# Edge counts per node: one-hot columns of width 128 replaced by products of two digits of eight pairs each

## The reference, cut to what matters

```python
def _gcn_norm(edge_index):
    loop = jnp.arange(N)
    src = jnp.concatenate([edge_index[0], loop])
    dst = jnp.concatenate([edge_index[1], loop])
    deg = jax.ops.segment_sum(jnp.ones_like(dst, jnp.float32), dst, num_segments=N)
    dinv = deg ** (-0.5)
    norm = dinv[src] * dinv[dst]
    return src, dst, norm
...
h = h @ W
msg = h[src] * norm[:, None]
out = jax.ops.segment_sum(msg, dst, num_segments=N) + b
```

## Time and profile before

| | us |
|---|---|
| median of three runs | 5987.89 (5987.56 to 5988.58) |
| time of the profiled execution | 5985.42 |
| its span, first to last instruction | 5983.6 |
| mean granted PE clock | 0.758 of full |
| stage `edge_tables` | 0 to 54.4 |
| stage `degrees` | 54.4 to 155.4 |
| stage `first_table` | 155.4 to 204 |
| stage `gcn` | 204 to about 3340 |

### The profile page before, as it was taken

How to read it: one execution, slowest core, us unless ns; L and a number is a source line. 1 busy time by engine, 2 the same in 40 slices (tenths; PEclk the granted TensorE clock), 3 DMA queues, 4 the chain that set the end, 5 groups by cost and what they waited for, 6 DMA issues and landing times. The chain is left out here.

```text
span 5983.6 us, 101443 instructions
## 1 busy us (share of the span) xinstructions
PE 4448.4 (74%) x24203; PEld 3115.8 (52%) x24204; DVE 3008.1 (50%) x7622; ACT 2469.0 (41%) x6463; POOL 3450.6 (58%) x3585
## 2 busy tenths in 40 slices
PE   5477777767777776667667649999957777777898
PEld 4254545433444443334333449999945555555566
DVE  7544444444444444333333533333358778878745
ACT  0544444434344443333333324444444444444221
POOL 0477777777777776777777452222237776766001
PEclk6577777766666666666666659999978888888899
DMA  4677777767777776777777552222144443333101
GB/s 128 192 198 196 197 197 196 198 183 201 206 201 204 203 201 185 192 196 192 196 192 196 161 181 35 35 37 35 34 145 115 114 108 106 106 106 96 56 1 43
DMA packets 550732, 862.18 MB, mean 144 GB/s; under 512 B 210941, under 2 KB 398326, under 8 KB 550422
## 3 DMA queue, kind: packets, MB, share of 16 engines
q0 software_dynamic: 219840, 641.37, 40.5%
q1 hardware_dynamic: 330710, 218.97, 12.3%
HBM read 709.79 MB, written 150.21 MB: 144 GB/s over the span
## 5 line engine op out<-in xcount | busy, mean ns | idle before, releaser
L1024 POOL DMA_INDIRECT rows<-node_limbs,psrc x2496 | 2366.0, 948 | 832.2 <-issue 567.0
L1299 PE MATMUL ps<-rows,hot 128*128 128x257 bf16 x7488 | 1638.0, 365 | 874.4 <-DMA rows<-node_limbs,psrc 728.6
L1088 DVE TENSOR_TENSOR shared<-shared,ps 128x257 f32 x2496 | 1056.4, 423 | 1639.5 <-PE ps L1299 1332.1
L1299 PEld LDWEIGHTS ps<-rows,hot 128*128 128x128 bf16 x7488 | 772.0, 122 | 1673.4 <-DVE shared L1088 825.4
L2234 POOL DMA_INDIRECT rows<-attn_table,psrc x832 | 789.8, 949 | 385.7 <-issue 222.7
L1213 ACT ACTIVATE away<-iota_f,pdl 128x128 f32<-128x128 f32 x2496 | 759.2, 387 | 46.5 <-PE ps L1299 46.2
L2541 PE MATMUL ps<-rows,hot 128*128 128x264 f32 x1664 | 583.1, 500 | 231.8 <-DVE rows L2335 175.7
L2541 PEld LDWEIGHTS ps<-rows,hot 128*128 128x128 f32 x1664 | 370.8, 239 | 362.1 <-issue 174.0
L1870 POOL DMA_INDIRECT resid<-feat,slot_node x105 | 164.1, 1563 | 622.4 <-DVE feat L1885 619.6
L2356 DVE TENSOR_TENSOR sums<-sums,ps 128x264 f32 x832 | 356.8, 429 | 113.1 <-PE ps L2541 42.5
L1987 PEld LDWEIGHTS ps<-feat 128*128 128x128 f32 x3360 | 393.2, 193 | 8.3 <-DVE feat L1914 2.4
(11 more groups left out here) (466 smaller groups left out, 5298.8 us busy)
## 6 DMA issues: line engine op xcount, KB each, us to landing
slot_rows<-blank SPq DMA_DIRECT2D x450, 130.0 KB
rows<-node_limbs,psrc POOLq DMA_INDIRECT x2496, 3.3
feat<-in_edge_attr_dram SPq DMA_DIRECT2D x832, 32.0 KB
node_limbs<-limbs SPq DMA_DIRECT2D x99, 196.0 KB, 3.9
feat<-slot_rows SPq DMA_DIRECT2D x105, 130.0 KB
rows<-attn_table,psrc POOLq DMA_INDIRECT x832
node_limbs<-limbs SPq DMA_DIRECT2D x12, 784.0 KB, 3.6
w<-in_L_ffn_W_dram SPq DMA_DIRECT2D x8, 1024.0 KB, 11.6
```

The costliest lines, as they stand in the source:

```text
L1024: g.indirect_dma_start(rows[:, n % RING, :], None, tables[k % 2], bass.IndirectOffsetOnAxis(ap=psrc[:, n:n + 1], axis=0)).then_inc(row_sem ...
L1088: v.tensor_tensor(row, row, ps[banks(k, i)[h * G + b]][:, 0:F + 1], ALU.add).then_inc(added.h, 1)
L1299: mm = pe.matmul(ps[cycle[s]][:, 0:F + 1], hot[:, 2 * half + h, b, :], rows[:, s, m * LIMB:m * LIMB + F + 1], start=(m == 0), stop=(m == 2))
```

## The change

A destination inside its tile, 0 to 127, is written as 8 x high + low, high being 0 to 15 and low 0 to 7. Eight pairs form a group (104 groups). For each group `hot_hi` holds 16 x 8 = 128 columns (high digit by pair) and `hot_lo` 8 x 8 = 64 columns (low digit by pair). One matmul per group, 128 columns stationary and 64 moving, gives all 16 x 8 x 8 x 8 combinations; only those where both pairs are the same are wanted. Eight groups fill a PSUM bank (13 fills, four banks in turn), and ACT copies each to `crossed` in bf16. Then 64 matmuls, one for each low digit and pair, take one column of each of the 104 groups as stationary operand and 16 columns of an identity as moving one, which leaves counts with the group on the partition. Eight matmuls with `hit` sum them per node tile.

The one-hots are made in two halves (7 fills and 6 fills) by 24 `tensor_scalar` comparisons each, in place of 52 `tensor_tensor` comparisons. The copies of the tile numbers go from DVE to ACT, the computation of `change` to POOL (with a subtraction, a square and a minimum for the comparison), the copies of the picked counts to ACT. `see_rows` takes 34 tiles early and 15 later. `iota_rep` is gone. SP's wait for the stored x moves from the end of `degrees` to `gcn`, ahead of the loop that reads it.

```diff
-    SEEN_EARLY = 22
+    SEEN_EARLY = 34
...
-                    v.tensor_copy(iota_rep[:], iota_f[:].rearrange("p (n j) -> p n j", j=1).to_broadcast([P, P, 2 * G]))
...
+        LO = 8
+        HI = P // LO
+        GROUPS8 = NPAIR // G
+        FILL = 512 // (LO * G)
+        FILLS = GROUPS8 // FILL
+        BANKS = 4
+        HALVES = [(0, FILLS // 2 + 1), (FILLS // 2 + 1, FILLS)]
...
-                    sp.wait_ge(x_kept.h, 16)
...
+                    g.memset(differs[:, 0:1], 1.0).then_inc(first_set.h, 1)
+                    g.memset(change[:, :, 0:1], -BIG).then_inc(change_set.h, 1)
+                    g.wait_ge(row_kept.h, 2)
+                    g.tensor_tensor(differs[:, 1:PCOL], tile_row[:, 1:PCOL], tile_row[:, 0:PCOL - 1], ALU.subtract).then_inc(differ_set.h, 1)
+                    g.wait_ge(first_set.h, 1)
+                    g.wait_ge(differ_set.h, 1)
+                    g.tensor_tensor(differs, differs, differs, ALU.mult).then_inc(differ_set.h, 1)
+                    g.wait_ge(differ_set.h, 2)
+                    g.tensor_scalar(change[:, :, 1:AG + 1], differs[:, 0:NPAIR].rearrange("p (n j) -> p n j", j=AG), 1.0, -BIG, ALU.min, ALU.mult).then_inc(change_set.h, 1)
...
-                    def mark(i, k):
-
-                        v.tensor_tensor(hot[:, k], iota_rep[:],
-                                        pdl_b[:, bass.ds(i * 2 * G, 2 * G)].rearrange("p (n j) -> p n j", n=1).to_broadcast([P, P, 2 * G]),
-                                        ALU.is_equal).then_inc(hot_ready.h, 1)
...
+                    v.tensor_copy(dst_i, pdl[:, 0:NPAIR])
                     v.drain()
+                    v.tensor_scalar(hi_i, dst_i, 3, None, ALU.arith_shift_right)
+                    v.drain()
+                    v.tensor_copy(hi_f, hi_i)
+                    v.tensor_copy(hi_b[:], hi_i)
+                    v.drain()
+                    v.scalar_tensor_tensor(lo_b[:], hi_f, -float(LO), pdl[:, 0:NPAIR], ALU.mult, ALU.add)
+                    v.drain()
+
+                    def mark(h):
+
+                        lo, hi = (FILL * f for f in HALVES[h])
+                        for part, hot, many in ((hi_b, hot_hi, HI), (lo_b, hot_lo, LO)):
+                            for j in range(many):
+                                op = v.tensor_scalar(hot[:, lo:hi, j * G:(j + 1) * G], part[:, lo * G:hi * G].rearrange("p (g n) -> p g n", n=G), float(j), None, ALU.is_equal)
+                        op.then_inc(hot_ready.h, 1)
+
+                    mark(0)
+                    v.tensor_copy(drow_f, prow[0:1, :]).then_inc(row_ready.h, 1)
+                    mark(1)
                     v.wait_ge(col_ready.h, 1)
+                    v.tensor_copy(dcol[0:GROUPS8, :], ps[7][0:GROUPS8, 0:G])
+                    v.drain()
+                    v.tensor_tensor(hit[0:GROUPS8], ...).then_inc(hit_ready.h, 1)
+                    see_rows(v, SEEN_EARLY, NT)
+                    share_stats(v, x_stats, x_mean, x_var, x_rstd, x_tmp, 0, NT)
...
+                    def keep(f):
+
+                        a.wait_ge(filled.h, f + 1)
+                        a.activation(crossed[:, f * 512:(f + 1) * 512], ps[f % BANKS][:], ACT.Copy).then_inc(fill_out.h, 1)
+
+                    a.activation(ident_b[:], ident[:], ACT.Copy).then_inc(ident_ready.h, 1)
+                    for f in range(*HALVES[0]):
+                        keep(f)
+                    a.wait_ge(col_ready.h, 1)
+                    a.activation(tile_row[:, 0:512], ps[5][:], ACT.Copy).then_inc(row_kept.h, 1)
+                    a.activation(tile_row[:, 512:PCOL], ps[6][:, 0:PCOL - 512], ACT.Copy).then_inc(row_kept.h, 1)
+                    for f in range(*HALVES[1]):
+                        keep(f)
+                    for h, bank in enumerate((ps[4], ps[1])):
+                        a.wait_ge(cnt_turned.h, h + 1)
+                        a.activation(cnt_t[0:GROUPS8, h * G // 2:(h + 1) * G // 2, :]..., bank[0:GROUPS8, :]..., ACT.Copy).then_inc(cnt_back.h, 1)
...
+                    def count(f):
+
+                        if f >= BANKS:
+                            pe.wait_ge(fill_out.h, f - BANKS + 1)
+                        for g in range(FILL):
+                            mm = pe.matmul(ps[f % BANKS][:, g * LO * G:(g + 1) * LO * G], hot_hi[:, f * FILL + g, :], hot_lo[:, f * FILL + g, :], start=True, stop=True)
+                        mm.then_inc(filled.h, 1)
...
+                    pe.wait_ge(ident_ready.h, 1)
+                    pe.wait_ge(fill_out.h, FILLS)
+                    by_column = crossed[:].rearrange("p (g c) -> p c g", c=LO * G)
+                    pick = ident_b[:].rearrange("p (a n) -> p n a", n=G)
+                    for n in range(G):
+                        bank = ps[4] if n < G // 2 else ps[1]
+                        for b in range(LO):
+                            at = n % (G // 2) * P + b * HI
+                            mm = pe.matmul(bank[0:GROUPS8, at:at + HI], by_column[:, b * G + n, :], pick[:, n, :], start=True, stop=True)
+                        if n % (G // 2) == G // 2 - 1:
+                            mm.then_inc(cnt_turned.h, 1)
+                    pe.wait_ge(hit_ready.h, 1)
+                    for n in range(G):
+                        if n % (G // 2) == 0:
+                            pe.wait_ge(cnt_back.h, n // (G // 2) + 1)
+                        mm = pe.matmul(ps[7][:, P:P + NT], cnt_t[0:GROUPS8, n, :], hit[0:GROUPS8, n, :], start=(n == 0), stop=(n == G - 1))
                     mm.then_inc(deg_ready.h, 1)
...
+                    sp.wait_ge(x_kept.h, 16)
                     with sp.Fori(0, NT) as j:
                         load_x(j)
```

More of the change, by code:

```diff
@@ L586, in _ @@
-                    mark(0, 0)
-                    mark(1, 1)
-                    with v.Fori(1, ITERS // 2) as j:
-                        for k in range(2):
-                            v.wait_ge(hot_used.h, 2 * j + k - 1)
-                            mark(2 * j + k, k)
-                    v.wait_ge(col_ready.h, 1)
-                    v.tensor_copy(dcol[:], ps[7][:, 0:ETB]).then_inc(v_step.h, 1)
-                    v.wait_ge(v_step.h, v_step.next())
-                    v.tensor_copy(tile_row[:, 0:512], ps[5][:]).then_inc(v_step.h, 1)
@@ L604, in _ @@
-                    v.memset(change[:, :, 0:1], -BIG).then_inc(v_step.h, 1)
-                    v.wait_ge(v_step.h, v_step.next())
-                    v.tensor_scalar(change[:, :, 1:AG + 1], differs[:, 0:NPAIR].rearrange("p (n j) -> p n j", j=AG), -BIG, None, ALU.mult).then_inc(v_step.h, 1)
-                    v.wait_ge(v_step.h, v_step.next())
-                    for b in range(ETB):
-                        v.tensor_scalar(hit[:, b, :], iota_f[:, 0:NT], dcol[:, b:b + 1], None, ALU.is_equal).then_inc(v_step.h, 1)
-                        v.wait_ge(v_step.h, v_step.next())
@@ L635, in _ @@
                 def _(a):
-                    def keep(i, k):
-                        a.wait_ge(hot_used.h, i + 1)
-                        a.activation(cnt[:, bass.ds(i * 2 * G, 2 * G)], ps[k][:, 0:2 * G], ACT.Copy).then_inc(count_out.h, 1)
-                    a.wait_ge(cnt_cleared.h, 1)
-                    with a.Fori(0, ITERS // 2) as j:
-                        for k in range(2):
-                            keep(2 * j + k, k)
+                    def keep(f):
[11 more added lines that the diff above has]
+                        a.wait_ge(cnt_turned.h, h + 1)
+                        a.activation(cnt_t[0:GROUPS8, h * G // 2:(h + 1) * G // 2, :].rearrange("p n (a b) -> p n b a", b=LO),
+                                     bank[0:GROUPS8, :].rearrange("p (n b a) -> p n b a", b=LO, a=HI), ACT.Copy).then_inc(cnt_back.h, 1)
                     root.scalar(a)
@@ L648, in _ @@
                 def _(pe):
+                    def count(f):
[4 more added lines that the diff above has]
+                        mm.then_inc(filled.h, 1)
+                    pe.wait_ge(hot_ready.h, 1)
+                    for f in range(*HALVES[0]):
+                        count(f)
                     pe.wait_ge(row_ready.h, 1)
@@ L651, in _ @@
                     pe.matmul(ps[6][:, 0:PCOL - 512], ones[0:1, :], drow_f[:, 512:PCOL], start=True, stop=True)
-                    for b in range(ETB):
-                        mm = pe.matmul(ps[7][:, b:b + 1], drow_f[0:1, b * P:(b + 1) * P], ones[0:1, 0:1], start=True, stop=True)
+                    for n in range(G):
+                        mm = pe.matmul(ps[7][0:GROUPS8, n:n + 1], drow_f[:, 0:NPAIR].rearrange("p (g n) -> p n g", n=G)[:, n, :], ones[0:1, 0:1], start=True, stop=True)
                     mm.then_inc(col_ready.h, 1)
-                    def count(i, k):
-                        pe.wait_ge(hot_ready.h, i + 1)
-                        if not isinstance(i, int) or i >= 2:
-                            pe.wait_ge(count_out.h, i - 1)
-                        for b in range(2 * G):
```

(21 more changed lines are left out.)

66 lines of the change are left out of this document (27 added, 39 removed).

## The result

The changed kernel takes 5925.24 us (median of 4 runs, 5922.3 to 5928.33), the kernel before 5988.24 us (4 runs, 5987.56 to 5990.37). The ratio is 0.9895, with a 95% interval of 0.9883 to 0.9907: 63.0 us less. The forecast was 64.9 us less and 5923.0 us. The profiled execution took 5922.3 us, of which 5920.4 are the span.

The account below looks back on a forecast made before the run. DVE was taken to bound the old comparison loop and the new stage's end; ending `degrees` at 90.6 instead of 155.46 saves 64.9 us, so 5987.89 - 64.9 = 5923.0 us, with an 80% range of 5912 to 5934.

Parts of the forecast that it names:

- The sum: Whole kernel: `degrees` ends at 90.6 instead of 155.46, 64.9 us saved, all of it lasting to the end, 5923.0 us.
- PE or POOL ends the stage: End of `degrees`: named sign of being wrong, as DVE was to end it, PE 1.2 us ahead.
- Early statistics, head: Before and at start of `degrees`: twelve more L308, 4.0 us, hidden by the gather; head 3.7 us, first comparison at 58.2.
- Comparisons: DVE's one-hot halves: 0.30 us a comparison of 448 elements, priced from L606; half one 7.2 us, half two 6.5.
- Rival 1: DVE's comparisons at twice the forecast rate, everything 2.8 us earlier: 5920.2 us; chance 0.28.
- Counting and ACT's copies: Half one on PE and ACT: 0.067 us a matmul, 0.6 a copy; rows and columns 6.5, DVE waits 3.5 us.
- DVE behind it: DVE after the tile columns: `dcol` and `hit` 0.8, statistics 5.0, `share_stats` 4.8, `u_cols` 0.9 us; done at 87.5.
- PE's own chain: PE's picks at 0.067 us, 4.3 in all, ACT's last copy and four matmuls 1.1: 86.3; root's table load inside it.
- rival 3: PE's picks load slowly: at 0.23 us the total is 5932.2 us; PE bounds from 0.086 a pick; chance 0.10.
- Tail: End of `degrees`, L628 to L886: unchanged at 3.06 us, ending the stage at 90.6.
- POOL: POOL's three two-input operations in `degrees`: 8.5 us, from 77.1 to 85.7, nothing on the path up to 4 us more.
- SP and the stored x: SP's stores: `run_start` lands by 71.1, stored x at 87.4; waits cost nothing and no transfers collide.

Follow-up runs that it names:

- second kernel of experiment 10: Changed kernel with 128-column picks, straight ACT copy, tile rows and columns ahead of the counting, POOL waiting for the comparisons: 5914.24 us, ratio 0.9876.
- experiment 9: Changed kernel with 22 early statistics tiles instead of 34 and SP's wait for stored x back at the end of `degrees`: stage 39.77 us.
- experiments 2 to 5: Changed kernel with picks of 128 columns (stage 32.96 us), of 104 neighbouring columns (32.65), then two tables of column numbers and distances (0.061 to 0.226 us a pick).
- experiment 10: Two kernels: changed kernel with 128-column picks and straight ACT copy, 5916.08 us; then also tile rows and columns first and POOL waiting, 5914.24 us.
- experiment 11: The fastest kernel (128-column picks, straight copy, tile rows and columns first) without POOL's wait for the comparisons: stage 28.42 us, 1.05 longer.

## Why the prediction was right, step by step

**The sum** was right (5923.0 for 5925.24, saving 64.9 for 63.0), and so was, within the scatter of the executions, the claim that a microsecond of this stage is one of the whole (the second kernel of experiment 10 does not bear it out). The way there was right in places, and errors of both signs cancelled. Its claim on what ends the stage was wrong: it had DVE there, and named "PE or POOL ends the stage" as a sign of being wrong. PE ended it.

- *Early statistics, head*: the head took 3.63 us for 3.7. "Cost nothing; the cover is that gather" failed in the profiled execution: the gather was issued earlier than before (last issue 37.65 us, before 39.47), and the 12 tiles more held `pair_dst` back by 1.2 us (experiment 9); in `degrees` they brought nothing. The stage started 0.4 us later, at 54.95; its start lies between 53.9 and 55.4 us over all runs, and differs also with the clock in the transposes ahead of it.
- *Comparisons*: 0.19 us for 0.30, half one 4.5 for 7.2. The failing step is "the nearest row is L606": same operation, other type. Rival 1, at 0.28, is what happened here (0.30 against 0.19 is a factor of 1.6), and moved all that follows 2.7 us forward.
- *Counting and ACT's copies*: 3.17/56 = 0.057 a matmul with its load for 0.067, 0.50 us a copy for 0.6; rows and columns 6.2 us for 6.5; DVE's wait 4.88 us for 3.5, because half two was ready earlier. `dcol` came at 72.54, forecast 76.0.
- *DVE behind it*: ready at 84.7 for 87.5. From `dcol` on its work took 12.1 us for 11.5. Two things lengthened it: L287 and L288, which end only when POOL's L587 ends at 80.2 us, cost 0.56 (5.14 us from L282 to L621, and 4.58 in experiment 9, where they run later), and 0.45 us of idle stand ahead of L282; the forecast's own terms were 0.4 too high in the rest. The prediction had put POOL's cost at nothing.
- *PE's own chain*, the step that failed: "L661 is the nearest row, 0.067". The picks took 0.180 us each, 11.55 us for 4.3. L661 loads 128 columns, and just those load fast at any distance (experiments 2 to 5). That was rival 3, at a chance of 0.10: 0.180 lies between its turning point, 0.086, and its dear end, 0.23. Then "ACT's last copy and four matmuls 1.1": the copy took 2.43 us for 0.6, as its writes lie 16 bytes apart; L834 writes straight. In sum: the picks began at 76.6 us for 80.8, and took 7.2 us more, the copy 1.8 more; 86.3 - 4.2 + 7.2 + 1.8 = 91.1. `deg` came at 91.07 us by PE's chain, and not at 87.5 by DVE's.
- *Tail*: 3.65 us for 3.06. ACT's late copy pushes the table load (1.28 us) behind `deg`: "the table load lies inside it" held no longer. In experiment 10, where the copy is early, the tail is 3.08 us again.
- *POOL* 6.6 us for 8.5, *SP and the stored x* as said: landed 88.5 us for 87.4, and nobody waited.

The arithmetic of the cancelling, at the stage's end: forecast 90.6; start and head +0.4; comparisons, counting, copies and rows bring `dcol` forward by 3.8 in all, so `dcol` is at 76.0 + 0.4 - 3.8 = 72.6, and with the 0.6 behind it DVE's own work ends at 84.7 and not 87.5. PE's chain ends 6.4 us after that, and the tail takes 3.6: 84.7 + 6.4 + 3.6 = 94.7, 4.1 us later than forecast. The stage alone thus saves 155.46 - 94.72 = 60.7 us, the medians 63.0. For the 2.3 us between them no trace shows a place; they are no more than executions of one kernel differ by (6 us over the four runs). So the closeness of the total is in part luck: by the stage the forecast was 4 us too low in time. By the prediction's own prices rival 1 is 2.8 us less and rival 3 at 0.180 us a pick is 6.0 more, (0.180 - 0.086) x 64: both together make 5926.2, and both together is what happened.

## What to carry to other kernels

When the nearest row of a trace prices an operation, compare type, number of columns and distance of elements, and the clock, not the opcode alone: each of the first three changed a price by a factor of 1.6 to 4 here. Give TensorE its stationary operand in full 128 columns, even if some are waste, when they lie 16 bytes or more apart, and let the matmul put its output in the order that the copy out of PSUM wants. A step costed at nothing because DVE was the bound (POOL's work, the table load) has to be looked at again once another engine's chain is the bound, and one costed at nothing because a wait covers it (the statistics) wants that wait looked at in more than one execution.

## What was not expected of the hardware

- A weight load of 127 columns, 64 bytes apart, took 0.226 us, one of 128 columns 0.061 us. Below 128 columns the price is 1.7 to 1.9 ns for each piece of 16 bytes touched, with and without transfers and, at 104 columns 128 bytes apart, at a clock of 0.50 and 0.77, as long as that is more than the packed load takes: 104 columns side by side 0.087 us at a clock of 0.50, 0.050 at 0.98.
- ACT's copy out of PSUM, 104x512: 0.60 us straight, 0.74, 1.30, 2.43, 2.30 with the bf16 elements 4, 8, 16, 32 bytes apart, 1.07 with f32 elements 16 bytes apart. Matmul outputs 32 bytes apart in PSUM showed no price behind these loads (11.56 for 11.55 us).
- DVE and POOL hold each other: 7.49 us for 1.68 on POOL beside the comparisons, 0.81 for 0.18 on DVE beside POOL. The Trainium skill, GPSIMD Engine Reference, section 1. Specifications, names contention with DVE operations in a two-port mode or with two inputs from SBUF. L287 and the comparisons, with one input, fit the first, though no trace shows an operation's mode. On the second the traces differ: `hit` in experiment 11, with two inputs, was held (1.80 us for 0.57), but L282 to L284, with two inputs and also beside L587, took 0.25, 0.24 and 0.24 us, and L282 without POOL had 0.25. Why these were not held stays open.
